# Attention row maxima: from a transpose on TensorE to a round trip through DRAM by DMA

## The chip, the cores and the metric

The kernel runs on one core of a Trainium2 chip. The metric is device time in microseconds of one execution, the median of several. Engines: TensorE (PE in the rows, with its weight loads as PEld), VectorE (DVE), ScalarE (ACT), GpSimd (POOL) and SyncE (SP), which here only issues DMAs.

## The reference

Two sequences of 2048 tokens, width 192, go through a quantised embedding, a layer norm with attention of 12 heads of 64, and a second layer norm with a mixture of small experts. The change is in the attention:

```python
scores = jnp.einsum('bqhe,bkhe->bhqk', q, k) / math.sqrt(D_HEAD)
scores = jnp.where(causal[None, None], scores, -jnp.inf)
pattern = jax.nn.softmax(scores, axis=-1)
z = jnp.einsum('bhqk,bkhe->bqhe', pattern, v)
attn_out = jnp.einsum('bqhe,hed->bqd', z, W_O) + b_O
```

The softmax needs, for each query, the largest score over its keys.

## The kernel before

The attention stage works in 12 units (`UNITS`), one for each pair of heads of each sequence; unit 6 begins the second sequence. Queries are cut into four chunks of 512 (`Q` = 0 to 3), keys into blocks of 128. A unit has two passes. The first pass of unit n projects q, k and v (`project`), and computes scores with queries on the partitions (`score_rows`, items "s1"); VectorE reduces each piece to maxima (`take_maxima`). When a chunk of 512 queries is complete, `maxima` writes the negated maxima, split into a high part and a rest, into columns of the tile `cpad`, one query per partition. `turn_maxima` (item "rows") turns these on TensorE, four 128x128 transposes, and ScalarE copies the 128x512 result into the tile `rows` (it is `zst`), where they lie along the free axis. The second pass (`score_columns`, items "s2") computes the scores again with keys on the partitions; its first matmul of each head multiplies ones with `rows` and so subtracts the maximum of every query. ScalarE takes the exponential (`exponentials`), GpSimd adds the columns up, TensorE multiplies with v (`weigh`).

The first pass of unit n+1 runs as side items inside the second pass of unit n. A unit's second pass has 40 key blocks, taken two at a time in 20 steps (`MACROS`); `sides` says which side items follow the two s2 items of each step. All items of TensorE that fill banks go round a ring of three pairs of PSUM banks (`RING`): item m waits until item m-3 was taken by the engine that reads it. The four "rows" items of a unit are in that ring: three among the s1 items, the fourth (Q = 3) in step 0 of the unit that uses it. The order of every engine is written out by these loops, and all run in order.

SyncE issues the loads in one stream. In its loop, step n loads the weights of unit n+2 and, at n = 5, first `load_x(1)`: the transposed activations of the second sequence into `xt_hi` and `xt_lo`, 1.5 MB in three DMAs. The projections of unit 6 read them; these are the side items of step 1 of unit 5.

Of the kernel before, what the change touches and what calls it, by code (L numbers as in the profile page):

```python
# [60 lines left out]
def tower(nc, x, tok_w, w_q, b_q, w_k, b_k, w_v, b_v, w_o, b_o,  # L61
          f_p, f_c, f_w1, f_b1, f_w2, f_b2, f_g1, f_g1b, f_g2, f_g2b, out, stages=3):
    ctx = ExitStack()
    with ctx:
# [12 lines left out]
        zst = sb("zst", [P, 2, NQ, GTOK], F32R)  # L77
        z_dram = nc.dram_tensor("z_scratch", (2, P, GTOK), F32, kind="Internal").ap()
# [4 lines left out]
        if stages >= 2:  # L83
            stage_attention(nc, w_q, b_q, w_k, b_k, w_v, b_v, w_o, h_all, ident, psum, banks, xT_dram,
                            f_p, f_c, f_w1, f_b1, pm_hi, pm_lo, w1c, zst, z_dram)
# [299 lines left out]
def stage_attention(nc, w_q, b_q, w_k, b_k, w_v, b_v, w_o, h_all, ident, psum, all_banks, xT_dram,  # L385
                    f_p, f_c, f_w1, f_b1, pm_hi, pm_lo, w1c, zst, z_dram):
# [14 lines left out]
    with ExitStack() as own:  # L401
# [21 lines left out]
        cpad = sb("cpad", [P, TQ, P])  # L423
# [13 lines left out]
        raw_c = cpad[:, :, :].rearrange("p t e -> p (t e)")[:, 0:NQ * M].rearrange("p (q m) -> p q m", m=M)  # L437
# [8 lines left out]
        max_taken, c_ready, rows_copied = sem("max_taken"), sem("c_ready"), sem("rows_copied")  # L446
# [16 lines left out]
        TAKEN = {"q": low_taken, "k": low_taken, "v": v_taken, "s1": max_taken, "rows": rows_copied,  # L463
# [12 lines left out]
        def first_pass(n):  # L476

            items = [(kind, n, c) for c in range(2) for kind in "qk"] + [("v", n, c) for c in range(2)]
            for i, c in CHUNKS:
                items.append(("s1", n, i, c))  # L480
                if i % TQ == 0 and i and c == i // TQ:
                    items.append(("rows", n, i // TQ - 1))
            return items

        def sides(it):

            plan = [[] for _ in range(MACROS)]
            plan[0].append(("rows", it, NQC - 1))
# [67 lines left out]
        def _(sp):  # L556
# [34 lines left out]

            load_x(0)
            for n in range(2):
                load_weights(n)
                load_wo(n)
            for n in range(UNITS):
# [13 lines left out]
            sp.wait_ge(filled, place[("rows", LAST, NQC - 1)] + 1)  # L610
# [22 lines left out]
        def _(pool):  # L633
            pool.memset(mask[:, :], 0.0).then_inc(mask_ready, 1)
# [32 lines left out]
        def _(pe):  # L667
# [48 lines left out]
            def turn_maxima(n, Q):  # L716
                banks = slot_free(place[("rows", n, Q)])
                pe.wait_ge(c_ready, n * NQC + Q + 1)
                for t in range(TQ):
                    last = pe.transpose(banks[0][:, t * P:(t + 1) * P], cpad[:, t, :], ident[:, :])  # L720
                last.then_inc(filled, 1)

            def score_columns(it, j):
# [3 lines left out]
                if kt == 0:  # L727
                    pe.wait_ge(rows_copied, it * NQC + Q + 1)
# [67 lines left out]
            def side(item):  # L796
# [6 lines left out]
                elif item[0] == "rows":  # L803
                    turn_maxima(*item[1:])
# [1077 lines left out]
```

## Time and profile before

| | us |
|---|---|
| median of 3 runs | 2665.2 (2664.42 to 2665.51) |
| profiled execution, whole | 2675.88 |
| its span | 2674.1 |
| TensorE busy | 2390.4 |
| VectorE busy | 1856.7 |
| ScalarE busy | 1237.7 |
| GpSimd busy | 1240.0 |
| attention stage | about 236 to 1815 |

A span runs from the first to the last instruction; an engine's busy time is the time in which at least one of its instructions ran. The share of busy time is a mean over three stages; the attention has to be looked at by itself.

### The profile page before, as it was taken

Reading aid. Unit: us, or ns where it says so; the run is one execution under the profiler, and the core shown is the slowest. Engines: PE = TensorE matmul, PEld = TensorE weight load, DVE = VectorE, ACT = ScalarE, POOL = GpSimd, SP = SyncE. Lnnn points to the kernel's source line nnn. Section 1 sums busy time; section 2 is a strip of 40 time slices with the busy share of each in tenths; the row PEclk is TensorE's granted clock in tenths of the full one; section 3 lists DMA queues with packets and bytes.
Section 4 is the critical chain, followed back from the end, with each engine's and each line's share of the span. In section 5 each row is a group of like instructions: output and inputs, shape, how many; then the busy total and the mean of one; then the engine's idle time right before and its main releaser. Section 6 shows DMA issues by size and latency. Waiting matters only on the chain. (4 is left out here: it accounts for less than half of the span.)

```text
span 2674.1 us, 42236 instructions
## 1 busy us (share of the span) xinstructions
PE 2390.4 (89%) x16000; PEld 1225.1 (46%) x16000; DVE 1856.7 (69%) x3768; ACT 1237.7 (46%) x1752; POOL 1240.0 (46%) x858
## 2 busy tenths in 40 slices
PE   2555899999999999999999999996899898998998
PEld 1222465655555555555555556543333333333332
DVE  4782765656565656565555656687888888888987
ACT  3332133333333333333333333355777787777776
POOL 5000166667575757575757666662413413324120
PEclk9877999999999999999999999996999999999999
DMA  1002000000001000000000001131000000000000
GB/s 49 12 13 64 8 8 1 10 1 9 8 2 33 1 10 1 9 1 9 1 9 1 3 1 20 19 52 55 9 19 21 15 19 21 15 19 9 19 7 7
DMA packets 42940, 39.33 MB, mean 15 GB/s; under 512 B 26865, under 2 KB 35186, under 8 KB 41842
## 3 DMA queue, kind: packets, MB, share of 16 engines
q1 hardware_dynamic: 40608, 31.18, 5.2%
q0 software_dynamic: 1536, 3.15, 0.4%
q8 instruction: 127, 2.08, 0.3%
q10 hardware_dynamic: 594, 2.31, 0.2%
q14 instruction: 75, 0.61, 0.1%
HBM read 26.13 MB, written 10.49 MB: 14 GB/s over the span
## 5 line engine op out<-in xcount | busy, mean ns | idle before, releaser
L663 POOL TENSOR_TENSOR acc<-acc,pT 128x1024 f32<-128x1024 f32 (+3 forms) x412 | 836.8, 2031 | 239.9 <-ACT pT L1062 203.5
L1062 ACT ACTIVATE pT<-banks 128x1024 f32<-128x1024 f32 x480 | 407.2, 896 | 811.9 <-PE banks L736 742.2
L1791 DVE TENSOR_TENSOR hw<-hid,banks 128x512 f32<-128x512 f32 x1024 | 663.3, 680 | 93.1 <-PE banks L1475 67.8
L881 DVE TENSOR_REDUCE part<-banks 128x2 f32<-128x1024 f32 (+3 forms) x432 | 438.2, 1044 | 312.0 <-PE banks L712 310.2
L1633 ACT ACTIVATE hid<-banks 128x1024 f32<-128x1024 f32 x512 | 496.8, 1022 | 188.6 <-PE banks L1465 167.3
L752 PE MATMUL banks<-pT,v 128*64 128x512 f32 (+3 forms) x1920 | 405.3, 543 | 1.1 <-POOL pT L647 1.1
L1475 PE MATMUL banks<-wT,select 64*128 64x512 f16 x1024 | 342.3, 395 | 38.2 <-DVE hw L1791 17.2
L1465 PE MATMUL banks<-zst,w1c 50*128 50x512 f32 x1024 | 306.9, 546 | 22.1 <-ACT hid L1633 22.1
L1483 PE MATMUL banks<-hw,w 128*32 128x512 f32 x2048 | 277.9, 615 | 0.8 <-DVE hw L1791 0.8
L1475 PEld LDWEIGHTS banks<-wT,select 64*128 64x128 f16 x1024 | 93.6, 94 | 393.0 <-DVE hw L1791 332.3
L752 PEld LDWEIGHTS banks<-pT,v 128*64 128x64 f32 x1920 | 116.6, 136 | 203.0 <-issue 180.9
L732 PE MATMUL banks<-zst,ones 64*128 64x512 f32 x960 | 199.6, 411 | 2.9 <-DVE h_all L939 2.7
L647 POOL TENSOR_SCALAR_AFFINE_SELECT pT<-pT 128x256 f32<-128x256 f32 x192 | 81.5, 425 | 244.7 <-ACT pT L1062 244.5
L712 PE MATMUL banks<-w1c 64*128 64x512 f32 (+3 forms) x1440 | 177.5, 375 | 10.6 <-DVE part L881 4.8
L736 PE MATMUL banks<-w1c 64*128 64x512 f32 (+3 forms) x1440 | 182.6, 361 | 0.0
L732 PEld LDWEIGHTS banks<-zst,ones 64*128 64x128 f32 x960 | 90.1, 183 | 197.8 <-issue 131.1
L924 DVE RECIPROCAL total<-total 128x256 f32<-128x256 f32 x96 | 167.6, 1746 | 3.1 <-ACT total L1070 2.7
L1375 POOL TENSOR_TENSOR o<-o,h_all 128x768 f32<-128x768 f32 x8 | 14.5, 1818 | 305.7 <-ACT o L1652 305.7
L712 PEld LDWEIGHTS banks<-w1c 64*128 64x128 f32 x1440 | 123.5, 186 | 50.1 <-ACT pT L1062 15.6
L1465 PEld LDWEIGHTS banks<-zst,w1c 50*128 50x128 f32 x1024 | 131.1, 194 | 28.6 <-ACT hid L1633 24.9
L736 PEld LDWEIGHTS banks<-w1c 64*128 64x128 f32 x1440 | 128.5, 185 | 17.9
L885 DVE CUSTOM_DVE_ANT_0 banks<-banks,mask 128x128 f32<-128x128 f32 x384 | 103.5, 312 | 29.3 <-PE banks L712 29.3
(225 smaller groups left out, 3167.3 us busy)
## 6 DMA issues: line engine op xcount, KB each, us to landing
zst<-z_scratch SPq DMA_DIRECT2D x48, 128.0 KB, 4.0
z_scratch<-zp SPq DMA_DIRECT2D x8, 512.0 KB, 2.8
out_h<-o SPq DMA_DIRECT2D x8, 384.0 KB, 2.6
xT_scratch<-xs_hi SPq DMA_DIRECT2D x4, 512.0 KB, 2.7
xt_hi<-xT_scratch SPq DMA_DIRECT2D x2, 1024.0 KB, 5.7
w<-in_L_ffn_W ACTq DMA_DIRECT2D x1, 2048.0 KB, 8.0
xt_hi<-in_L_ffn_W SPq DMA_DIRECT2D x12, 128.0 KB, 4.5
v<-in_L_ffn_W SPq DMA_DIRECT2D x12, 128.0 KB, 4.3
```

The source lines that it names most:

```text
L663: pool.tensor_tensor(acc[:, G % 2, :, off:CH], acc[:, G % 2, :, off:CH], pT[:, slot, :, 0:w], ALU.add).then_inc(summed, 1)
L712: last = pe.matmul(banks[h][:, 0:w], a[u][head(h), i * P:(i + 1) * P], b[u][head(h), c * CH:c * CH + w], start=(k == 0), stop=(k == 2))
L732: pe.matmul(banks[h][:, 0:w], ones[head(h), :], rows[head(h), u, Q, off:CH], start=True, stop=False)
L736: last = pe.matmul(banks[h][:, 0:w], a[u][head(h), kt * P:(kt + 1) * P], b[u][head(h), t0:t0 + w], start=False, stop=(k == 2))
L752: last = pe.matmul(psum[6 + G % 2][head(h), off:CH], v[:, u, kt, head(h)], pT[:, J % PSLOTS, h, 0:CH - off], start=(kt == 0), stop=(j == L ...
L881: last = dve.tensor_reduce(to[:, :, c:c + 1], both[:, :, 0:whole], AX.X, ALU.max)
L1062: act.activation(pT[:, J % PSLOTS, :, 0:CH - off], both[:, :, 0:CH - off], ACT.Exp, scale=E ** -0.5)\
L1465: last = pe.matmul(psum[i], w1[rows, s % NQ, j * P:(j + 1) * P], zst[rows, g % 2, s % NQ, :], start=True, stop=True)
L1475: pe.matmul(bank, select[rows, jr, :], wT[rows, g % 2, s, :], start=True, stop=True).then_inc(spread, 1)
L1483: last = pe.matmul(psum[Y][32 * i:32 * i + 32, :], w2[:, s, j, :], hw[:, n % 2, i, :], start=(n == 0), stop=(n == NSTEP - 1))
L1633: act.activation(hid[:, n % 2, 2 * pair:2 * pair + 2, :], banks[:, pair * 1024:(pair + 1) * 1024].rearrange("p (q n) -> p q n", n=GTOK), A ...
L1791: dve.tensor_tensor(hw[:, n % 2, q, :], hid[:, n % 2, q, :], ring_bank(("w", g, n, q)), ALU.mult).then_inc(mixed, 1)
```

## The change

The "rows" items are gone from TensorE, from ScalarE and from the ring. `maxima` writes its values into a small tile `shift_parts` (two slots, four values for each query of a tile). SyncE stores a slot in DRAM and loads it back in another order, straight into partitions 0, 1, 64 and 65 of `rows`; the other partitions are set to zero once by GpSimd at the beginning. The matmul that uses the rows waits for the load. `raw_c`, which lay in `cpad`, has its own tile, and SyncE no longer waits for the last "rows" item before it loads it.

```diff
+        shift_parts = sb("shift_parts", [P, 2, TQ, 4], F32R)
+        raw_c = sb("raw_c", [P, NQ, M])
...
                 items.append(("s1", n, i, c))
-                if i % TQ == 0 and i and c == i // TQ:
-                    items.append(("rows", n, i // TQ - 1))
...
-            plan[0].append(("rows", it, NQC - 1))
...
+            def turn_maxima(n, Q):
+                G = n * NQC + Q
+                slot, earlier = G % 2, G // 2
+                sp.wait_ge(c_ready, G + 1)
+                sp.dma_start(shift_dram[slot].rearrange("t p k -> p t k"), shift_parts[:, slot, :, :].bitcast(F32))\
+                  .then_inc(parts_stored[slot], 16)
+                sp.wait_ge(parts_stored[slot], 16 * earlier + 16)
+                if n >= 2:
+                    sp.wait_ge(filled, place[("s2", n - 2, NK - 1)] + 1)
+                if earlier:
+                    sp.wait_ge(rows_in[slot], 32 * earlier)
+                else:
+                    sp.wait_ge(rows_cleared, 1)
+                    for h in range(2):
+                        sp.dma_start(rows[h * E:h * E + 2, n % 2, Q, :].bitcast(F32),
+                                     shift_dram[slot, :, :, 2 * h:2 * h + 2].rearrange("t p k -> k (t p)"))\
+                          .then_inc(rows_in[slot], 16)
...
+            for Q in range(NQC):
+                turn_maxima(0, Q)
             for n in range(UNITS):
...
+                if n < LAST:
+                    for Q in range(NQC):
+                        turn_maxima(n + 1, Q)
...
-            sp.wait_ge(filled, place[("rows", LAST, NQC - 1)] + 1)
...
+            pool.memset(rows[:, :, :, :].bitcast(F32), 0.0).then_inc(rows_cleared, 1)
...
                 if kt == 0:
-                    pe.wait_ge(rows_copied, it * NQC + Q + 1)
+                    G = it * NQC + Q
+                    pe.wait_ge(rows_in[G % 2], 32 * (G // 2) + 32)
...
-            pe.wait_ge(consts_ready, 3)
+            pe.wait_ge(consts_ready, 2)
+            pe.wait_ge(rows_cleared, 1)
...
             def maxima(n, Q):
-                if n or Q:
-                    before = ("rows", n, Q - 1) if Q else ("rows", n - 1, NQC - 1)
-                    dve.wait_ge(filled, place[before] + 1)
-                leading, rest = (cpad[:, :, k:k + E + 1:E] for k in range(2))
+                G = n * NQC + Q
+                if G >= 2:
+                    dve.wait_ge(parts_stored[G % 2], 16 * (G // 2))
+                high, rest = (shift_parts[:, G % 2, :, k:k + 3:2] for k in range(2))
...
-            def copy_rows(n, Q):
-                both = item_in(("rows", n, Q))
-                act.activation(rows[:, n % 2, Q, :], both[:, 0, :], ACT.Copy).then_inc(rows_copied, 1)
```

TensorE at the beginning of unit 2, with what each instruction waits for, before the change (L720 is the item "rows", L736 the scores of the second pass, L752 the product with v):

```order
L736 MATMUL banks<-qh,kl 128x384 x2
L720 MATMUL banks<-ident,cpad 128x128 [waits c_ready,max_taken]
L720 MATMUL banks<-ident,cpad 128x128 x3
L752 MATMUL banks<-pT,v 64x256 [waits masked,exp_done]
L752 MATMUL banks<-pT,v 64x256
```

and at the same place in the changed kernel, where L754 stands for L736, L770 for L752 and L750 for L732:

```order
L754 MATMUL banks<-qh,kl 128x384 x2
L770 MATMUL banks<-pT,v 64x256 [waits masked,exp_done]
L770 MATMUL banks<-pT,v 64x256
L770 MATMUL banks<-pT,v 64x128 [waits masked,exp_done]
L770 MATMUL banks<-pT,v 64x128
L784 MATMUL banks<-acc,ones_half 64x512 [waits summed,max_taken]
```

The four transposes and their two waits are gone; nothing stands in their place.

SyncE's stream from the load of the output weights of unit 5 to the second sequence's activations, before:

```order
L579 DMA wo<-in_L_attn_W_O 128x192 [waits ring_filled]
L558 DMA xt_hi<-xT_scratch 128x2048
L560 DMA xt_lo<-xT_scratch 64x1024 x2
L569 DMA w_hi<-in_L_attn_W_Q 128x2x64
L569 DMA w_lo<-in_L_attn_W_Q 64x2x64 x2
```

and in the changed kernel:

```order
L578 DMA wo<-in_L_attn_W_O 128x192 [waits ring_filled]
L596 DMA shift_scratch<-shift_parts 128x4x4 [waits c_ready]
L607 DMA zst<-shift_scratch 2x512x1 [waits rows_in_a,ring_filled,parts_stored_a]
L607 DMA zst<-shift_scratch 2x512x1
L596 DMA shift_scratch<-shift_parts 128x4x4 [waits c_ready]
L607 DMA zst<-shift_scratch 2x512x1 [waits rows_in_b,ring_filled,parts_stored_b]
...
L607 DMA zst<-shift_scratch 2x512x1 [waits rows_in_b,ring_filled,parts_stored_b]
L607 DMA zst<-shift_scratch 2x512x1
L557 DMA xt_hi<-xT_scratch 128x2048 [waits v_taken,low_taken]
L559 DMA xt_lo<-xT_scratch 64x1024 x2
```

The three loads of the activations stand behind the four round trips of unit 5's maxima, and so behind the wait for its last maxima.

## Rows read from the trace of the kernel before

**Rows 1.** Stretch inside the attention (us, then busy us of each engine, granted clock, DMA)
```profile
core 0: us, PE busy (x) PEld busy (x) DVE busy (x) ACT busy (x) POOL busy (x), PEclk, DMA share, GB/s
560.00:680.00 120.00, 117.60 (x830) 69.66 (x830) 72.48 (x131) 39.80 (x50) 77.08 (x54) 1.00 0.03 6
```

**Rows 2.** Groups of instructions by line (busy us, mean ns, idle before, releasers)
```profile
L720 PE MATMUL banks<-ident,cpad 128*128 128x128 f32 x192 | 31.4, 286 | 5.4 <-DVE cpad L900 3.4 <-DVE part L881 2.0
L1053 ACT ACTIVATE zst<-banks 128x512 fp32r<-128x512 f32 x48 | 28.7, 598 | 38.5 <-PE banks L720 38.5
```

**Rows 3.** Timeline of TensorE, steady state (start us, us, what)
```profile
442.91 0.66 PE L720 MATMUL banks<-ident,cpad 128*128 128x128 f32 x4
...
488.40 0.66 PE L720 MATMUL banks<-ident,cpad 128*128 128x128 f32 x4
489.30 0.98 PE L712 MATMUL banks<-w1c 64*128 64x512 f32 x6 [0.25 <-ACT pT L1062]
...
697.01 0.66 PE L720 MATMUL banks<-ident,cpad 128*128 128x128 f32 x4
697.60 0.87 PE L752 MATMUL banks<-pT,v 128*64 128x256 f32 x8
```

**Rows 4.** Waits by engine and line, 440 to 1700 us (total us, times, longest)
```profile
PE banks L712 <- ACT pT L1062: 5.0, 20, 0.3
```

**Rows 5.** Timeline, end of the first pass of unit 0, beginning of its second
```profile
303.94 3.97 DVE L881 TENSOR_REDUCE part<-banks 128x2 f32<-128x1024 f32 x4 [1.23 <-PE banks L712]
...
319.16 0.63 PE L720 MATMUL banks<-ident,cpad 128*128 128x128 f32 x4 [1.90 <-DVE cpad L900]
```

**Rows 6.** Timeline, beginning of unit 5
```profile
950.48 0.18 DVE L900 TENSOR_TENSOR cpad<-negmax,cpad 128x8 fp32r<-128x8 f32 x1
951.00 0.66 PE L720 MATMUL banks<-ident,cpad 128*128 128x128 f32 x4
954.30 1.55 PE L696 MATMUL banks<-xt_hi,w_hi 128*128 128x512 f32 x3
```

**Rows 7.** Timeline of SyncE's queue, the activations of the second sequence
```profile
854.95 0.38 SPq L558 DMA_DIRECT2D xt_hi<-xT_scratch  x1
855.37 1.13 SPq L560 DMA_DIRECT2D xt_lo<-xT_scratch  x2
```

**Rows 8.** DMA issues, 850 to 880 us (KB each, us from issue to landing)
```profile
xt_lo<-xT_scratch SPq DMA_DIRECT2D x2, 256.0 KB, 6.7
wo<-in_L_attn_W_O SPq DMA_DIRECT2D x1, 96.0 KB, 1.8
bk<-in_L_attn_b_K SPq DMA_DIRECT2D x1, 0.5 KB, 2.1
```

**Rows 9.** DMA packets, 481.0 to 481.8 us: only 4-byte ones, of the two bias loads
```profile
DMA packets 208, 0.00 MB, mean 1 GB/s; under 512 B 208, under 2 KB 208, under 8 KB 208
q1 hardware_dynamic: 208, 0.00, 11.9%
```

**Rows 10.** DMA packets, 474.8 to 475.4 us: mostly 256-byte ones, weights
```profile
DMA packets 288, 0.08 MB, mean 127 GB/s; under 512 B 272, under 2 KB 288, under 8 KB 288
q1 hardware_dynamic: 288, 0.08, 53.7%
```

**Rows 11.** TensorE's restart at the beginning of the attention, a stretch as in rows 1
```profile
244.00:254.00 10.00, 6.09 (x9) 2.08 (x10) 0.00 (x0) 0.28 (x1) 0.00 (x0) 0.51 0.31 67
```

**Rows 12.** Timeline of the same beginning, GpSimd and TensorE
```profile
236.28 0.20 POOL L634 MEMSET mask<- 128x128 f32 x1 [188.74 <-POOLq L109]
...
247.91 2.90 PE L696 MATMUL banks<-xt_hi,w_hi 128*128 128x512 f32 x3 [17.73 <-DMA bv_bc<-in_L_attn_b_V]
```

**Rows 13.** Group of instructions: GpSimd's memset of zst in the next stage
```profile
L1302 POOL MEMSET zst<- 32x2048 f32 x2 | 3.6, 1800 | 0.1
```

More of the change, by code:

```diff
@@ L84, in tower @@
             stage_attention(nc, w_q, b_q, w_k, b_k, w_v, b_v, w_o, h_all, ident, psum, banks, xT_dram,
-                            f_p, f_c, f_w1, f_b1, pm_hi, pm_lo, w1c, zst, z_dram)
+                            f_p, f_c, f_w1, f_b1, pm_hi, pm_lo, w1c, zst, z_dram, shift_dram)
         if stages >= 3:
@@ L385, in stage_attention @@
 def stage_attention(nc, w_q, b_q, w_k, b_k, w_v, b_v, w_o, h_all, ident, psum, all_banks, xT_dram,
-                    f_p, f_c, f_w1, f_b1, pm_hi, pm_lo, w1c, zst, z_dram):
+                    f_p, f_c, f_w1, f_b1, pm_hi, pm_lo, w1c, zst, z_dram, shift_dram):
     CH = 512
@@ L445, in stage_attention @@
         hi_done, low_taken, v_taken = sem("hi_done"), sem("low_taken"), sem("v_taken")
-        max_taken, c_ready, rows_copied = sem("max_taken"), sem("c_ready"), sem("rows_copied")
+        max_taken, c_ready, rows_cleared = sem("max_taken"), sem("c_ready"), sem("rows_cleared")
+        parts_stored, rows_in = [sem("parts_stored_a"), sem("parts_stored_b")], [sem("rows_in_a"), sem("rows_in_b")]
         exp_done, masked, summed = sem("exp_done"), sem("masked"), sem("summed")
@@ L462, in stage_attention @@
         CHUNKS = [(i, c) for i in range(KT) for c in range(i // TQ + 1)]
-        TAKEN = {"q": low_taken, "k": low_taken, "v": v_taken, "s1": max_taken, "rows": rows_copied,
+        TAKEN = {"q": low_taken, "k": low_taken, "v": v_taken, "s1": max_taken,
                  "s2": exp_done, "total": total_copied, "out": out_added, "x2": xt_taken, "z": xt_taken}
@@ L590, in load_part @@
                       .then_inc(w1_in[q % 2], 16)
+            def turn_maxima(n, Q):
[11 more added lines that the diff above has]
+                    sp.wait_ge(rows_cleared, 1)
+                with nc.allow_non_contiguous_dma(reason="single values, in the background"):
+                    for h in range(2):
+                        sp.dma_start(rows[h * E:h * E + 2, n % 2, Q, :].bitcast(F32),
+                                     shift_dram[slot, :, :, 2 * h:2 * h + 2].rearrange("t p k -> k (t p)"))\
+                          .then_inc(rows_in[slot], 16)
             load_x(0)
@@ L714, in score_rows @@
                 last.then_inc(filled, 1)
[L716 to L721, printed above, removed]
             def score_columns(it, j):
@@ L802, in side @@
                     make_z()
-                elif item[0] == "rows":
-                    turn_maxima(*item[1:])
                 elif item[0] == "out":
@@ L835, in _ @@
             dve.memset(ones_half[:, :], 1.0).then_inc(consts_ready, 1)
-            dve.memset(cpad[:, :, :], 0.0).then_inc(consts_ready, 1)
             dve.wait_ge(mask_ready, 2)
@@ L892, in maxima @@
             def maxima(n, Q):
-                if n or Q:
-                    before = ("rows", n, Q - 1) if Q else ("rows", n - 1, NQC - 1)
-                    dve.wait_ge(filled, place[before] + 1)
-                leading, rest = (cpad[:, :, k:k + E + 1:E] for k in range(2))
+                G = n * NQC + Q
+                if G >= 2:
+                    dve.wait_ge(parts_stored[G % 2], 16 * (G // 2))
+                high, rest = (shift_parts[:, G % 2, :, k:k + 3:2] for k in range(2))
                 link(dve.tensor_reduce(negmax[:, :], part[:, Q % 2, :, :], AX.X, ALU.max, negate=True))
                 by_tile = negmax[:, :].rearrange("p (t h) -> p t h", h=2)
-                link(dve.tensor_copy(leading.bitcast(F32R), by_tile))
-                dve.tensor_tensor(rest.bitcast(F32R), by_tile, leading, ALU.subtract).then_inc(c_ready, 1)
+                link(dve.tensor_copy(high, by_tile))
+                dve.tensor_tensor(rest, by_tile, high.bitcast(F32), ALU.subtract).then_inc(c_ready, 1)
             def sum_odd(j):
@@ L986, in keep_part @@
                 if q is None:
-                    part, raw = cm[:, :, :], raw_c
+                    part, raw = cm[:, :, :], raw_c[:, :, :]
                 else:
@@ L1091, in side @@
             def side(item):
-                if item[0] == "rows":
-                    copy_rows(*item[1:])
-                elif item[0] == "x2":
+                if item[0] == "x2":
                     take_x2(item[1])
```

5 lines of the change are left out of this document (2 added, 3 removed).

## The prediction

> **What bounds the kernel now.** I read first the stretches of the attention, then the groups of instructions that the change touches, then the timelines around them, and last SyncE's queue and the DMA packets. In a stretch of 120 us in the middle of the attention [rows 1] the reader should see TensorE busy 117.6 us at a granted clock of 1.00, while VectorE has 72.5, ScalarE 39.8 and GpSimd 77.1 us of work. So here the length is TensorE's own list of instructions, and what leaves this list shortens the stage. The unit repeats every (697.01 - 442.91) / 2 = 127.05 us, since these two "rows" items are the same one, two units apart [rows 3].
>
> **What goes.** There are 192 transposes in 48 items, 31.4 us of TensorE, and 48 copies, 28.7 us of ScalarE [rows 2]. The copies lie beside TensorE's work and are worth nothing by themselves. For TensorE not the busy time counts but the place that an item takes: from its start to the next one's start is 697.60 - 697.01 = 0.59 us, call it 0.58 [rows 3]. Three of the 48 items lie in the first pass of unit 0. The other 45 give 45 x 0.58 = 26.1 us. At some of them the next item comes 0.90 us later and not 0.58 (488.40 to 489.30, rows 3), because its bank is still with the exponential; the waits name 20 of these, 5.0 us together, all that this line has between 440 and 1700 us [rows 4]. Without the "rows" item the same bank is asked for one item later, after a longer score item, so I count these 5.0 us as gone too. They could come back before another item; the bound is 0 to 6.
>
> In unit 0 the first pass is held by VectorE, not TensorE. What the item cost there is VectorE's gap of 1.23 us at the third one, and in step 0 of the second pass TensorE's own wait of 1.90 us for `c_ready` [rows 5]. Part of this is taken up by what comes behind; I count 2, bounds 0 to 4. Sum of what goes: 26.1 + 5.0 + 2 = 33 us, bounds 26 and 36.
>
> **What is added and costs nothing.** The GpSimd memset of `zst` holds TensorE by a wait. Two memsets over 2048 columns take 1.80 us each [rows 13], so 4096 columns are 3.6 us from 236.3, done at 240; TensorE begins at 247.91, held by the first loads [rows 12]. It has 8 us of cover. Work of VectorE stays as it was: the two small instructions of `maxima` write another tile. SyncE has room, since a round trip is a store of 512 packets and two loads of 1024. A rows load is due early: those of chunks 0 to 2 are asked for in the next unit, those of chunk 3 in step 12 of 20, some 75 us behind `c_ready`. The load of the experts' weights moves behind the last round trip, from unit 10 to the beginning of unit 11, and is wanted in its steps 8 and 9, about 50 us later, so it is covered too unless the round trips are several times longer than below.
>
> **What is added and lies on the path.** SyncE's stream is in order, and `load_x(1)` now stands behind the round trip of unit 5's last maxima. Before, it was issued at 854.95 [rows 7], 99 us ahead of the projections that read it. Now it can't be issued before the maxima are ready at 950.66, and the projection of unit 6 is asked for at 954.30 - 0.58 = 953.7 [rows 6]. TensorE is in order, so everything stands behind it: unit 5's scores, and with them ScalarE and GpSimd. Step by step:
> - The store: a load of 128 small packets lands in 2.1 us [rows 8]; 384 more packets at 0.6 us / 288 = 2.1 ns [rows 10] are 0.8 us. It lands at 953.6.
> - The two loads of single values: no DMA of before is like this one (2 partitions, 1024 packets of 4 bytes each). The nearest row is the 4-byte packets of the bias loads, 208 in 0.8 us, or 3.85 ns each over all engines [rows 9]: 2048 of them are 7.9 us. From below: their busy share is 11.9%, that is 0.119 x 16 x 800 / 208 = 7.3 ns of an engine per packet, so that 16 engines could do 2048 in 0.9 us. From above: one engine saw such a packet every 16 x 800 / 208 = 61.5 ns, and if few engines carry them they take up to 63 us (below). I take 7.9, the row of the same size of packet.
> - The activations, issued at about 954.8: before, the second `xt_lo` was issued at 855.9 and landed 6.7 us later [rows 7, 8], 7.7 us behind the first issue. By themselves they land at 962.5; behind the packets, in the same queue, at 970.4. I take the second.
> - So TensorE stands 970.4 - 953.7 = 16.7 us, bounds 8.8 and 50 and more.
> - The clock: at the beginning of the attention, after a wait of 17.73 us, TensorE worked from 247.91 to about 254 at the lower level, 1.2 GHz (clock 0.51 in that stretch), before it was back at 2.4 [rows 11, 12]. Six microseconds at half are 3 lost; I count 3, bounds 0 and 5.
>
> **The sum.** -33 + 16.7 + 3 = -13.3 us. Against the profiled execution, 2675.9, that is 2662.6; that execution was 10.7 us above the median of the runs, 2665.2, and against this I forecast **2652 us**. Its own range: 2638 (36 gone, 8.8 of stall, no clock) to 2660.
>
> **How many engines carry the single values.** The loads' destination has two partitions, and the before kernel has none like it: its smallest has 16. The Trainium skill (DMA: Bandwidth & Descriptors, "Why a DMA increments its semaphore by 16 and not by 1") says that a DMA is spread over the largest number up to 16 that divides the slowest dimension of both patterns: here 2. No run here shows it yet. By that rule each round trip gives two engines 1024 packets each; at the 7.3 ns of busy time [rows 9] this is 7.5 us, as in my sum, and at the pace an engine showed with 16 in use it is the rival below.
>
> **The rivals.**
> - *A longer stall, gain given back.* The packets of single values take T instead of 7.9 us, for want of engines or for HBM reads that wait for each other; the stall is 8.8 + T. From T = 21 us (8.8 + 21 + 3 = 33), or 20 ns a packet on two engines, the kernel isn't faster any more. At T = 30 it is 2665.2 - 33 + 38.8 + 3 = 2674 us. For it: 256-byte packets come every 16 x 600 / 288 = 33 ns on an engine at the densest [rows 10]. Against: they were busy 17.9 ns of it, 4-byte ones only 7.3.
> - *The round trips become the bound (slower).* Place: SyncE's queue in every unit. It decides from the point at which four round trips take more than a unit of 127 us, T = 31.8 us, or 31 ns a packet on two engines. At 33 ns, T = 34.1 and a unit takes 136.5, 9.5 more for some 11.5 units: 2775 us. At 61.5 ns, T = 63, 252 us a unit, +1440: 4100 us. For it: the pace of rows 9, and the rule above. Against: the bias loads were only 8 packets per engine, so the pace holds their start and end.
> - *The activations aren't held up by the packets.* The stall is 8.8, and the time 2665.2 - 33 + 8.8 + 3 = 2644 us. For it: engines that the single values don't use are free; against: the load is done only when its last share is.
> - *TensorE's freed time is not used.* Another engine or a bank wait takes the place; then only the stall remains, 2665.2 + 20 = 2685 us. Against it speak 77 of 120 us as the highest load of another engine [rows 1].
>
> **How the numbers follow.** My forecast 0.42, the short stall 0.10, the long stall 0.25, the round trips as the bound 0.17, the unused time 0.06. A difference under 0.2% (5.3 us, so 2660 to 2670.5) can't be told from none. Faster: 0.40 of the forecast, all of the short stall, 0.01 of the long: 0.51. Same: the rest of the forecast and 0.13 of the long stall: 0.16. Slower: 0.33. The range reaches from 2638 to 2680, which leaves out the round trips as the bound and the end of the unused time.
>
> **What would show it.** Right: no transposes of maxima on TensorE, units of 127.05 - 2.9 = 124.1 us; one idle time of TensorE of about 17 us before L720 (the projection) near 930 us, ended by the DMA of `xt_hi` or `xt_lo`; behind it some microseconds at the lower clock; the loads of `zst` from the scratch landing 8 to 12 us after their issue; no wait of the scores (L750) for them. Wrong: waits of L750 in every unit (the second rival), a single stall of 30 us or more (the first), units that stay at 127 us (the last).

## The result and the profile after

The changed kernel takes 2670.7 us (median of 20 runs, 2666.1 to 2674.3), the kernel before 2665.2 (20 runs beside them): a ratio of 1.0017, 95% interval 1.001 to 1.0024. It is a little slower, by about as much as a measurement can tell. The forecast was 2652.

The page of the kernel after, its head and busy times:

```profile
span 2670.0 us, 41959 instructions
PE 2375.1 (89%) x15808; PEld 1215.9 (46%) x15808; DVE 1867.8 (70%) x3767; ACT 1212.7 (45%) x1704; POOL 1245.2 (47%) x859
```

TensorE's busy time fell by 15 us and ScalarE's by 25, and the span by 4. (The spans flatter the change: in the execution profiled before the first projection began at 247.91 us [rows 12], after at 237.2, and the embedding stage ahead of it is the same in both.) Since TensorE works in order, I cut its timeline at the first projection of each unit, the same instruction every time:

```profile
430.52 1.12 PE L720 MATMUL banks<-xt_hi,w_hi 128*128 128x512 f32 x2
557.06 1.12 PE L720 MATMUL banks<-xt_hi,w_hi 128*128 128x512 f32 x2
682.12 1.13 PE L720 MATMUL banks<-xt_hi,w_hi 128*128 128x512 f32 x2
808.77 1.13 PE L720 MATMUL banks<-xt_hi,w_hi 128*128 128x512 f32 x2
```

The reader should see units of 126.5, 125.1 and 126.7 us where before had 127.0 [rows 3] and the forecast 124.1. One unit is far longer, 144.6 us (808.77 to 953.40), the one with the load of the second sequence. There TensorE's timeline, SyncE's queue and the landings (KB each, us from issue to landing) read:

```profile
935.29 0.28 PE L754 MATMUL banks<-qh,kl 64*128 64x128 f32 x2
953.40 3.42 PE L720 MATMUL banks<-xt_hi,w_hi 128*128 128x512 f32 x4 [17.84 <-issue]
```
```profile
932.44 0.36 SPq L596 DMA_DIRECT2D shift_scratch<-shift_parts  x1
935.41 4.01 SPq L607 DMA_DIRECT2D zst<-shift_scratch  x2
939.53 4.13 SPq L557 DMA_DIRECT2D xt_hi<-xT_scratch  x1
943.70 1.16 SPq L559 DMA_DIRECT2D xt_lo<-xT_scratch  x2
```
```profile
xt_hi<-xT_scratch SPq DMA_DIRECT2D x1, 1024.0 KB, 9.8
xt_lo<-xT_scratch SPq DMA_DIRECT2D x2, 256.0 KB, 7.9
```

That is the stall of the forecast, 17.8 us for 16.7. Its inside differs: the two loads of single values hold the queue for 4.0 us while they are issued, and the issue behind them, of the activations, is held another 4.1 us, where the same one took 0.38 before [rows 7]. (In the diff ahead the two loads look as if they stood in the `else` branch. They are issued for every chunk, four times a unit.)

The waits of TensorE in the attention, 300 to 1750 us (total us, times, longest):

```profile
PE banks L795 <- DVE part L897: 23.6, 11, 2.2
PE banks L720 <- issue: 17.8, 1, 17.8
PE banks L736 <- DVE part L897: 7.8, 11, 0.7
PE banks L795 <- DVE oT L947: 1.8, 1, 1.8
```

No wait of L750 for the rows: the round trips are hidden, as forecast. The waits for ScalarE of [rows 4] are gone too. But there is one wait a unit of 2.1 us at the output (L795), and one of 0.7 at a score item (L736). The kernel before waited at the same output, 15.8 us in 11 units, at most 1.5 us. My text ahead had not looked at that line. This is one of these waits, first after, then before:

```profile
488.31 1.84 PE L736 MATMUL banks<-w1c 64*128 64x512 f32 x18
492.28 2.93 PE L795 MATMUL banks<-wo,oT 128*128 128x192 f32 x8 [2.13 <-DVE part L897]
```
```profile
504.92 1.84 PE L712 MATMUL banks<-w1c 64*128 64x512 f32 x18
508.21 1.57 PE L777 MATMUL banks<-wo,oT 128*128 128x192 f32 x8 [1.45 <-DVE part L881]
```

The same eight matmuls take 2.93 us for 1.57. Stretches of the kernel after around this place (columns as in [rows 1]) show why:

```profile
488.30:491.70 3.40, 1.84 (x20) 1.35 (x16) 3.30 (x6) 1.24 (x2) 2.87 (x2) 1.00 0.08 2
491.70:495.10 3.40, 2.82 (x8) 2.42 (x8) 2.16 (x6) 0.00 (x0) 1.85 (x1) 0.56 0.11 1
```

The granted clock is near the lower of the two levels, 1.2 GHz, in the second stretch. Such a drop of 3.4 us, each worth some 1.6 us, stands in nine of the ten units between 305 and 1588 us; before had none there. In steady state a unit with a drop takes 126.5 to 126.7 us, the one without 125.1.

What VectorE did before that output, with GpSimd beside it:

```profile
486.61 0.20 DVE L913 TENSOR_REDUCE negmax<-part 128x8 f32<-128x40 f32 x1
486.84 1.48 DVE L915 CAST shift_parts<-negmax 128x8 fp32r<-128x8 f32 x1
488.36 0.17 DVE L916 TENSOR_TENSOR shift_parts<-negmax,shift_parts 128x8 fp32r<-128x8 f32 x1
488.44 1.75 DVE L940 RECIPROCAL total<-total 128x256 f32<-128x256 f32 x1
490.22 0.69 DVE L947 TENSOR_TENSOR oT<-banks,total 128x512 f32<-128x512 f32 x1
491.00 2.36 DVE L897 TENSOR_REDUCE part<-banks 128x2 f32<-128x1024 f32 x2
```
```profile
483.38 4.91 POOL L687 TENSOR_TENSOR acc<-acc,pT 128x1024 f32<-128x1024 f32 x2 [0.91 <-ACT pT L1074]
```

Read it backwards. The output is item m of the ring and needs the banks of item m-3, a score item that VectorE frees with the first L897 reduction, at about 492.2. Ahead of it in VectorE's order stand the multiply, the reciprocal and the three small operations on the maxima. The CAST of 128x8 values takes 1.48 us and ends at 488.32, just as the second of GpSimd's two additions in that row does (483.38 + 4.91 = 488.29). At the same place before, the same CAST took 0.60 us:

```profile
503.65 0.60 DVE L899 CAST cpad<-negmax 128x8 fp32r<-128x8 f32 x1
```

Why did it collide now and not before? `sides` spreads the items of the next unit's first pass evenly over 16 steps, by their number. The change took three "rows" items out of that list, so 40 items are cut instead of 43, and score items that had nothing to do with the change moved by a step. Step 8 had (6,1), (7,0), (7,1) and has (7,0), (7,1); step 7 got (6,1). Item (7,1) completes chunk 1, and the maxima of chunk 1 are turned right behind it. They come sooner against GpSimd's addition, and the CAST is held by more of it.

### The profile page after: what moved, and what is told of

It reads as the page before. It is cut to its first block and busy times, and to the rows that moved or that the text cites. A ratio compares the mean times of both kernels' runs of the same rounds, so it can differ in the third digit from the quotient of the medians.

```text
span 2670.0 us, 41959 instructions
## 1 busy us (share of the span) xinstructions
PE 2375.1 (89%) x15808; PEld 1215.9 (46%) x15808; DVE 1867.8 (70%) x3767; ACT 1212.7 (45%) x1704; POOL 1245.2 (47%) x859
## 5 line engine op out<-in xcount | busy, mean ns | idle before, releaser
L897 DVE TENSOR_REDUCE part<-banks 128x2 f32<-128x1024 f32 (+3 forms) x432 | 437.2, 1044 | 295.5 <-PE banks L736 293.2
L770 PE MATMUL banks<-pT,v 128*64 128x512 f32 (+3 forms) x1920 | 410.6, 549 | 1.1 <-POOL pT L671 1.1
L770 PEld LDWEIGHTS banks<-pT,v 128*64 128x64 f32 x1920 | 118.1, 138 | 205.1 <-issue 170.8
L750 PE MATMUL banks<-zst,ones 64*128 64x512 f32 x960 | 200.0, 412 | 3.2 <-DVE h_all L955 2.7
L736 PE MATMUL banks<-w1c 64*128 64x512 f32 (+3 forms) x1440 | 177.2, 377 | 13.2 <-DVE part L897 9.0
L754 PE MATMUL banks<-w1c 64*128 64x512 f32 (+3 forms) x1440 | 182.9, 362 | 0.0
L750 PEld LDWEIGHTS banks<-zst,ones 64*128 64x128 f32 x960 | 90.1, 184 | 199.0 <-issue 129.3
L736 PEld LDWEIGHTS banks<-w1c 64*128 64x128 f32 x1440 | 124.4, 188 | 52.9 <-DVE part L897 18.7
L754 PEld LDWEIGHTS banks<-w1c 64*128 64x128 f32 x1440 | 128.3, 185 | 18.4
L720 PE MATMUL banks<-xt_hi,w_hi 128*128 128x512 f32 x192 | 98.5, 637 | 35.7 <-issue 17.8
```

What stands on the lines that cost most here:

```text
L736: last = pe.matmul(banks[h][:, 0:w], a[u][head(h), i * P:(i + 1) * P], b[u][head(h), c * CH:c * CH + w], start=(k == 0), stop=(k == 2))
L750: pe.matmul(banks[h][:, 0:w], ones[head(h), :], rows[head(h), u, Q, off:CH], start=True, stop=False)
L754: last = pe.matmul(banks[h][:, 0:w], a[u][head(h), kt * P:(kt + 1) * P], b[u][head(h), t0:t0 + w], start=False, stop=(k == 2))
L770: last = pe.matmul(psum[6 + G % 2][head(h), off:CH], v[:, u, kt, head(h)], pT[:, J % PSLOTS, h, 0:CH - off], start=(kt == 0), stop=(j == L ...
L897: last = dve.tensor_reduce(to[:, :, c:c + 1], both[:, :, 0:whole], AX.X, ALU.max)
```

## The experiments

All are compared with the kernel before on the same chip. In the names, x is the second sequence's activations, and the cut is the way in which the list of side items is divided over the steps; the numbered parts below explain each. Units are steady ones (a unit with a drop, where most have one), read as above. The drops are counted in the ten units from the first projection of unit 1 to that of unit 11; two that begin with the start of the first of these (in kept ahead and in before, new cut) are left out. The twelve kernels ahead of the last two ran where before took 2665 to 2666 us. For the last two before took 2676.4, and their own traces begin the attention at 248.7 and 250.2 us where the others have 236 to 239, so about 11 us more lie ahead of the attention, as in the execution profiled before. There the ratio counts.

| kernel | us | ratio, 95% interval | unit, us | drops in ten units |
|---|---|---|---|---|
| the changed kernel | 2670.7 | 1.0017 [1.001, 1.0024] | 126.6 | 9 |
| x ahead | 2652.8 | 0.9954 [0.994, 0.9967] | 126.6 | 8 |
| x between | 2657.5 | 0.9968 [0.9956, 0.998] | 126.6 | 6 |
| loads doubled | 2678.2 | 1.0048 [1.0034, 1.0061] | 126.6 | 6 |
| items kept | 2666.0 | 1.0002 [0.9993, 1.0011] | 127.0 | 0 |
| kept ahead | 2634.1 | 0.9882 [0.9867, 0.9897] | 124.1 | 0 |
| kept behind | 2661.6 | 0.9984 [0.9975, 0.9993] | 126.6 (128.2 with a drop) | 2 |
| old cut, x ahead | 2630.7 | 0.9869 [0.9854, 0.9884] | 124.2 | 0 |
| outputs later | 2627.4 | 0.9859 [0.9844, 0.9874] | 123.9 | 0 |
| no cast | 2652.4 | 0.9955 [0.9941, 0.9968] | 126.7 | 8 |
| old cut alone | 2650.3 | 0.995 [0.9936, 0.9964] | 124.2 | 0 |
| before, new cut | 2696.8 | 1.0117 [1.0102, 1.0133] | 129.7 | 9 |
| before, outputs later | 2642.6 | 0.9924 [0.991, 0.9938] | 125.05 | 0 |
| maxima behind | 2619.6 | 0.9784 [0.977, 0.9797] | 122.3 | 0 |
| outputs later, old cut | 2621.1 | 0.9787 [0.9774, 0.9801] | 122.4 | 0 |

**1. The stall: x ahead, x between, loads doubled.** The load of the second sequence moves ahead of unit 5's round trips; or between the last `c_ready` and its store; or stays, and each load of single values runs twice, the second time into an unused tile.

```diff
-                    if n == NP - 1:
-                        load_x(1)
...
+                if n == NP - 2:
+                    sp.wait_ge(low_taken, 4 * n + 8)
+                    sp.wait_ge(v_taken, 2 * n + 4)
+                    load_x(1)
                 if n < LAST:
                     for Q in range(NQC):
```

> The changed kernel with one move in SyncE's stream: the three loads of the second sequence's activations stand ahead of the four round trips of unit 5, behind the load of the output weights, as early as before. Theory (the stall of 17.8 us and the 1.5 us of slower matmuls behind it come from that place alone): both go, 2670.6 - 19.3 = 2651 us, up to 2653 if unit 5 gets the short clock drop that its neighbours have. Rival (the gain is lost to the DMA traffic or spread over the units): 2662 or more.

> The changed kernel, with the activations loaded behind the wait for unit 5's last maxima, but ahead of their round trip. This parts the stall in two. Theory (the wait for the maxima costs the rest, the packets of the round trip and SyncE's blocked issue the most): TensorE stands 5 to 6 us and not 17.8, the time is 2670.6 - 12 = 2658 us. Rival (the order against the packets does not matter, only the late issue): the stall stays above 12 us, 2666 us or more.

> The changed kernel with every load of single values done twice, the second time into an unused tile. Theory (the activations queue behind the packets, some 8 us per round trip; in all other units the round trips are hidden): the one stall grows from 17.8 to about 26 us, the units stay as they are, 2678 us. Rival 1 (packets of other loads do not hold the activations): 2671. Rival 2 (the packets cost the other units something): units longer than 126.7 us, 2690 or more.

All three came out as expected: 2652.8, 2657.5 and 2678.2. With x ahead TensorE's long wait is gone and no other wait changes by more than 0.5 us. Between, it is shorter; doubled, longer:

```profile
939.27 3.75 PE L722 MATMUL banks<-xt_hi,w_hi 128*128 128x512 f32 x4 [4.97 <-issue]
```
```profile
959.56 3.75 PE L728 MATMUL banks<-xt_hi,w_hi 128*128 128x512 f32 x4 [25.26 <-issue]
```

So two loads of 1024 single values cost 25.26 - 17.84 = 7.4 us, where the forecast took 7.9 for them. Doubled, they delay no other unit: four round trips don't come near a unit's length. The stall is worth 2670.65 - 2652.84 = 17.8 us. With x ahead the kernel should then have been at about 2632, had the forecast's other terms held; 20 us were still missing.

**2. Is it the items? Items kept, kept ahead, kept behind.** x ahead in all three, and at the places of the old items TensorE does four transposes of `ident` into the item's bank and ScalarE copies them to an unused tile. Kept are all four of a unit; those of chunks 3 and 0; those of chunks 1 and 2.

```diff
+                if i % TQ == 0 and i and c == i // TQ and i // TQ - 1 in KEPT:
+                    items.append(("rows", n, i // TQ - 1))
...
+            if NQC - 1 in KEPT:
+                plan[0].append(("rows", it, NQC - 1))
```

> The kernel of e1 with the items put back on TensorE and ScalarE: four transposes of the identity and a copy into an unused tile at the old places, waiting for the maxima as before, while the rows come by DMA. Theory (the DMA path is free in itself; the short clock drops belong to the new order of TensorE): units of 127.0 us as before, no drops in the attention, 2665 us. Rival (the DMA traffic brings the clock drops or slows TensorE): drops in the units, 2675 us or more.

> The kernel with the activations loaded first and the rows by DMA, with the unused transposes and copies kept at two of the four places of a unit only: chunks 3 and 0, the two that lie ahead of step 9, where TensorE waits for VectorE before the output item. Theory (freed time ahead of step 9 makes that wait longer, 2.13 against 1.45 us, and the short clock drop follows a wait of that length): the wait is 1.5 us again, no drops, units of about 125.8 us, 2652 us. Rival (the drops come from fewer instructions on TensorE as such, or at other places): drops in most units, 127 us a unit, 2662 or more.

> The same with the unused transposes and copies kept at the other two places, chunks 1 and 2, which lie behind step 9. Theory: the wait of step 9 stays 2.1 us and the drops stay, units of about 127.8 us, 2665 us. Rival: no drops, units of about 126, 2652 us.

With all four kept the time and the unit are those of before, and no clock drops: with x ahead the DMA path itself costs TensorE nothing. But kept ahead gave 2634.1, 19 us faster than none kept, where 2652 was expected and 2662 or more by the rival. An item that costs 0.58 us can't save 1.7 us a unit. What the edit also does is to change the number of items in the list, 41 here. That cut puts (7,1) into step 9, the step of the output itself, three items ahead of it. So the output needs the banks of (7,1), which VectorE frees before it turns the maxima, and the wait falls from 2.1 us to this:

```profile
616.04 1.57 PE L811 MATMUL banks<-wo,oT 128*128 128x192 f32 x8 [0.16 <-DVE part L919]
```

Kept behind missed too. Its list has 42 items, and (7,1) stays in step 8, but (8,0) joins it there. The wait of 2.1 us was expected to stay, with the drops, and 2665 us. Instead there are two shorter waits close together in each unit, 0.71 and 1.23 us, and the time is 2661.6. Two of the ten units have the drop even so. This is one of them; in the others the same eight matmuls take 1.54 us:

```profile
618.35 0.50 PE L745 MATMUL banks<-kh,qh 64*128 64x512 f32 x2 [0.71 <-DVE part L915]
620.83 2.49 PE L811 MATMUL banks<-wo,oT 128*128 128x192 f32 x8 [1.23 <-DVE oT L965]
```

**3. The cut by itself.** The items stay gone; placeholders stand in the list where they were, and are dropped after cutting. With x ahead, and as the only edit of the changed kernel. And the reverse in the kernel before: its score items cut as the change cuts them, the "rows" items behind the same score items as ever.

```diff
                 items = first_pass(it + 1)
+                for Q in range(NQC - 1):
+                    items.insert(items.index(("s1", it + 1, TQ * (Q + 1), Q + 1)) + 1, None)
...
-                    plan[t] += rest[a:z]
+                    plan[t] += [item for item in rest[a:z] if item]
```

> The kernel with the activations first, and with the score items of the first pass at exactly the steps where they stood before the change (the list is cut as if the three removed items were still in it). Theory (the place of the score items plays no part, VectorE's lateness in step 9 does): wait of step 9, drops and time as with the activations first, 2653 us. Rival (the new cut is what brings the drops): no drops, units of 125.0 us, 2639 us.

> The changed kernel with one edit: the score items of the next unit are issued at the steps where they stood before the change (x stays behind the round trips, as changed). Theory (the two losses are separate and add): the cut is worth 2652.84 - 2630.69 = 22.2 us with x ahead, of which the ten or so drops of the clock; the long stall of unit 5 stays at 17.8 us, so 2670.7 - 22 = 2648.5, faster than before by 0.6%. Rival (the gain of the old cut is bound to x being ahead): 2665 to 2671.

> The kernel before with one edit, the other way round: its 40 score items are cut into the 16 steps without counting the three items that turn the maxima, as the change cuts them; these stand behind the same score items as ever. Nothing is removed. Theory (the new cut alone makes VectorE late at step 9, since its cast meets the beginning of GpSimd's addition): the wait of 1.45 us becomes 2.1 and the clock drops behind it in most units, 11 times 0.7 plus about 10 times 1.6, so 2665.5 + 22 = 2687. Rival (the items that turn the maxima give VectorE the slack there, and the new cut hurts only without them): 2665.

With x ahead it is the rival that was right, and by more than it asked for: 2630.7, 22.2 us under x ahead. As the only edit it gives 2650.3, 20.3 us under the changed kernel and 0.5% under before. In the kernel before the new cut costs 31.7 us, more than the 22 expected, and brings the drops with it. There the wait of 2.1 us, and the drop behind it, stand at the "rows" item just ahead of the output; the expectation had left out the second wait, 0.7 us a unit. The three agree in sign: the cut of the score items costs 20 to 32 us, with or without the change that brought it. The waits of the kernel with the old cut and x ahead:

```profile
PE banks L799 <- DVE part L901: 15.7, 11, 1.4
PE banks L799 <- DVE oT L951: 10.4, 12, 1.8
```

At the same output VectorE's cast is 0.61 us long, and the stretches around it keep the higher clock, although TensorE still waits 1.4 us there:

```profile
484.34 0.61 DVE L919 CAST shift_parts<-negmax 128x8 fp32r<-128x8 f32 x1
```
```profile
485.60:489.00 3.40, 1.96 (x21) 1.45 (x17) 3.33 (x5) 1.26 (x2) 2.86 (x2) 1.00 0.08 2
489.00:492.40 3.40, 3.40 (x18) 1.80 (x20) 2.45 (x6) 0.00 (x0) 1.87 (x1) 1.00 0.21 6
```

**4. The chain on VectorE: no cast, maxima behind.** x ahead and the new cut in both. One writes the high part with a maximum of the row with itself instead of a copy; the other turns the maxima of chunks 0 to 2 one score item later.

```diff
-                link(dve.tensor_copy(high, by_tile))
+                link(dve.tensor_tensor(high, by_tile, by_tile, ALU.max))
```
```diff
-                if diagonal and t == TQ - 1:
+                if c == 0 and t == 0 and Q or (i, c) == (KT - 1, NQC - 1):
                     dve.wait_ge(max_taken, nth[("s1", n, i, c)] + 1)
-                    maxima(n, Q)
+                    maxima(n, (i - 1) // TQ)
```

> x ahead of the round trips and the new cut, with one edit: VectorE writes the high part of the negated maxima with a maximum of the row with itself (a TENSOR_TENSOR, as the one that follows it, 0.17 us) instead of a copy (CAST). In the kernel with x ahead and the copy, the CAST of chunk 1 took 1.48 us and ended with GpSimd's addition, and TensorE waited 2.1 us for a pair of banks behind it, after which the clock dropped for 3.4 us. Theory (the cast holds VectorE until GpSimd's addition is over, that makes the wait long, and the long wait brings the drop): the wait falls to some 0.8 us, 1.3 us a unit less over 11 units (14), and the drops go, 9 to 11 times 1.6 us (14 to 18): 2652.8 - 28 to 32, thus 2621 to 2625. Rival (the new cut is late by its own load, and the kind of the instruction doesn't matter): 2653.

> x ahead of the round trips and the new cut, with one edit: VectorE turns the maxima of chunks 0 to 2 into their two parts one score item later, behind the first score item of the next chunk instead of ahead of the reciprocal and the multiply on which the output rests. Theory (the three operations, 0.20 + 1.48 + 0.17 us with their gaps 1.9 us, stand on VectorE ahead of all that the output's banks wait for; the copy is held until GpSimd's addition ends; the wait of 2.1 us that this makes brings the drop of the clock): the wait at the output falls by up to 1.9 us a unit and the drops go, so the unit of 126.65 comes down to 123.2 to 124 and the time to 2620 to 2628. Rival (the drops come from something else in that step, such as its load or GpSimd's addition beside it): the wait goes but the drops stay, 2652.5 - 4 to 21, thus 2632 to 2648.

The first changed nothing (2652.4): my theory that the copy is the kind that is held fell. The operation in its place is held just as long, until GpSimd's addition is over (484.12 + 4.91 = 489.03):

```profile
487.55 1.50 DVE L917 TENSOR_TENSOR shift_parts<-negmax 128x8 fp32r<-128x8 f32 x1
489.09 0.17 DVE L918 TENSOR_TENSOR shift_parts<-negmax,shift_parts 128x8 fp32r<-128x8 f32 x1
489.17 1.75 DVE L942 RECIPROCAL total<-total 128x256 f32<-128x256 f32 x1
```
```profile
484.12 4.91 POOL L689 TENSOR_TENSOR acc<-acc,pT 128x1024 f32<-128x1024 f32 x2 [0.92 <-ACT pT L1076]
```

The second, with the same operations, the same cut and the same number of instructions, took the unit from 126.6 (125.0 without a drop) to 122.3 us, the ratio from 0.9954 to 0.9784. The wait at the output is 0.4 us and no clock drops any more:

```profile
PE banks L797 <- DVE part L899: 4.5, 11, 0.4
PE banks L752 <- DVE h_all L957: 2.7, 2, 2.1
PE banks L797 <- DVE oT L949: 1.8, 1, 1.8
```

That is 45 us of the 2665, more than the 25 to 33 expected; again the expectation had left out the 0.7 us wait at a score item, which went too (7 us), and what lies behind the ten units gained as well (from the first projection of unit 11 to the end it is 1079.5 us for 1086.3). The list of operations is as it was; only what stands ahead of the freeing reduction moved, and both the wait and the drop went with it. One thing did change beside the order: at their new places the CASTs are held for less, 10.3 us in all for 39.0 with x ahead, so this run alone doesn't part the wait from the load. The next one does.

**5. The outputs later.** x ahead, and the output items of chunks 0 to 2 one step later, at the head of the step; the same in the kernel before; and with the old cut on top.

```diff
-        OUT_BEHIND = [4] * LAST + [6]
+        OUT_BEHIND = [5] * LAST + [6]
...
-                    plan[t].append(("out", it, Q))
+                    plan[t].insert(len(plan[t]) if it == LAST else 0, ("out", it, Q))
```

> The kernel with the activations first, and the output items of chunks 0 to 2 one step later and at the head of their step, where their bank was taken long before. Theory (the wait before the output item is lost time of TensorE and brings the drop): both go, 125.0 - 2.1 = 122.9 us a unit, 11 units: 2653 - 11 x 3.2 = 2618 us. Rival (VectorE is late for the score items too, so the wait moves to the next item): units above 124.5, 2640 or more.

> The kernel before with the output items of chunks 0 to 2 one step later and at the head of the step, in all units but the last, as was done to the changed kernel with x ahead (which this took from 2652.8 to 2627.4). Control: how much of that gain is there without the change. In the trace of before the outputs wait 15.8 + 3.4 + 1.8 = 21 us for banks, no clock drops stand in the attention, so at most 20 us can go: 2645 to 2650. Theory (the change is worth its 1.6 to 2 us a unit once nothing waits at the outputs): it ends some 18 to 22 us above 2627.4, at 2647. Rival (the gain of the kernel with outputs later came from the outputs alone and the change adds nothing): 2627.

> The best of what was found put together: x ahead of the round trips, the outputs one step later, and the score items at their steps of before. The kernel with the outputs later has waits of 0.70 and 0.28 us a unit left, both for VectorE's reductions, and the one with the old cut has neither. Theory (both go): 2627.4 - 11 x 0.98 = 2616.6. Rival (TensorE is at its own pace once no wait is over 1 us, or others take their place): 2625 to 2628.

With x ahead it took the time to 2627.4, between theory and rival: the output's waits and the drops are gone, two waits of 0.7 and 0.3 us a unit for VectorE's reductions are left. VectorE is as busy as with x ahead here (1867.2 us for 1867.9) and its CASTs are held as long (38.8 us for 39.0, 1.49 at this place). So the drops go with TensorE's wait, not with the load of that step. The kernel before gains too, 22.5 us (2642.6), where at most 20 were expected: 19 of the 21 us that its outputs had waited are gone, and 2.7 us of waits for ScalarE. With the old cut nothing waits in the middle of a unit, and the ratio is 0.9787. By the ratios that is 19 us under outputs later, for the 11 expected; the units are 1.5 us shorter for waits of 1.0, and where the other half comes from is open. Its longest line of waits for VectorE's reductions is this:

```profile
PE banks L740 <- DVE part L901: 2.2, 5, 1.0
```

This kernel and maxima behind are the fastest of the study, 2.1% under before; between them the measurement sees no difference.

The kernel before with the outputs later, and the changed one with the outputs later and the old cut, are also the cleanest measure of the change itself. They have the same cut, the same place of the outputs, and no waits of note; a steady unit of each, before first:

```profile
558.69 1.13 PE L696 MATMUL banks<-xt_hi,w_hi 128*128 128x512 f32 x2
683.84 1.13 PE L696 MATMUL banks<-xt_hi,w_hi 128*128 128x512 f32 x2
```
```profile
561.80 1.12 PE L724 MATMUL banks<-xt_hi,w_hi 128*128 128x512 f32 x2
684.20 1.12 PE L724 MATMUL banks<-xt_hi,w_hi 128*128 128x512 f32 x2
```

125.15 against 122.40. Over nine steady units the means are 125.05 and 122.40: 2.65 us a unit, for the 2.9 of the forecast.

## Why the prediction was wrong

Its sum had the terms -33 (what goes), +16.7 (the stall) and +3 (its clock). Each has a measured partner:

- *What goes, -33:* from all items kept to items gone with the old cut, x ahead in both, 2666.0 - 2630.7 = 35.3 us. Right in size. The stretch of unit 0 gave 4.6 us (72.9 to 68.3), of which 0.6 is its fourth item, so 4.0 where the forecast had 2. The 5.0 us of bank waits did go, as counted. What the parts leave out is that the outputs now wait for `oT`, 10.4 us for 1.8, so their agreement is in part luck.
- *The stall with its clock, +19.7:* with the old cut, x late against x ahead, 2650.3 - 2630.7 = 19.6 us; with the new cut 17.8. Right in size. Of its parts, the clock's share varies: in the changed kernel the first four matmuls behind the stall took 3.42 us for 1.98, 1.5 us lost and not 3; with the old cut the unit behind the stall is 2.6 us longer than its neighbours (126.8 for 124.2). The loads of single values cost 7.4 us for 7.9, but how they take it is not as in the forecast. In a dense stretch, 937 to 940 us, the profile of the changed kernel counts

```profile
DMA packets 1002, 0.00 MB, mean 1 GB/s; under 512 B 1002, under 2 KB 1002, under 8 KB 1002
q1 hardware_dynamic: 1002, 0.00, 18.8%
```

so one packet every 3.0 ns over all engines, each busy 0.188 x 16 x 3000 / 1002 = 9.0 ns and not 7.3, with 3.0 of them under way at a time. The Trainium skill's rule from the prediction (DMA: Bandwidth & Descriptors, "Why a DMA increments its semaphore by 16 and not by 1") gives two engines for each load. Two engines that take one packet after the other at 9 ns would need 9.2 us for 2048 packets; here either the packets overlap in an engine or the two loads of a pair are on different engines, and the trace doesn't say which. That 7.5 us came near is luck. The pace of 61.5 ns, on which the slow rival stood, was only that of a short load's start and end. What I had not seen is where the time is spent: SyncE's queue itself stands, in the issue of these loads and of the next one.
- *Missing, +20.3:* the new cut (2670.65 - 2650.34). This is the step that failed, a term that the sum has at nothing without giving a reason. The sum counted an item's place on TensorE and took it that "what leaves this list shortens the stage"; it held the other items to be where they were. The text ahead says of the side items only that `sides` places them. The comparison of the two instruction streams would have shown the score items moving by a step, and the waits of the kernel before that its outputs already stood 1.5 us behind VectorE in every unit. Either was to be had without a run.

The sum with it is -35.3 + 19.6 + 20.3 = +4.6, for +5.4 measured. The three differences form one chain of kernels, from items kept to the changed one, so they must add up to the distance between these two; what the sum tests is only that items kept is where before is. And the changed kernel with the old cut, the one that the forecast really described, took 2650.3 us for a forecast of 2652.

The chances have a slip: by their parts Same is 0.02 + 0.13 = 0.15 and Slower 0.34, not 0.16 and 0.33.

The rivals: the long stall, the round trips as the bound and the short stall are refuted by the stall of 17.8 us and by the doubled loads. The one on freed time that isn't used, with a chance of 0.06, named a bank wait as what could take the place, and a bank wait is what came. But it held the freed time to be lost, and that was not so: the items' 35 us came off, and the new cut took 20 back. I argued against it with VectorE's and GpSimd's busy shares, 72 and 77 of 120 us. These say nothing of a chain of 6 us in which one waits for the other in each unit, and they hardly grew: in the stretch of [rows 1] GpSimd has 77.5 us after for 77.1, VectorE 76.6 for 72.5. The price named there, 2685, stood for no gain at all; in truth 2.4 us a unit were taken back: against the kernel with the old cut (124.2 us) a unit has 2.1 + 0.7 us of waits for 1.4 + 0.8, and the drop's 1.6, which is 2.2 of the 2.4.

What each of these is worth alone is not separated fully. That the drops follow the waits, and not the load of the step, is shown by outputs later, where the load stays and both go, and by before, new cut, where the long wait stands at another item and the drop comes behind it. Which waits bring one is not settled. One of 2.1 us does in most units but not in all: in the changed kernel's unit from 557 to 682 us the wait is 2.15 us and the clock stays at 1.00, and x between and loads doubled have the same waits and 6 drops in ten units. One of 1.4 us did in none, and the pair of 0.71 and 1.23 us of kept behind did in two of ten. Why is open.

## What to carry to other kernels

When a change takes items out of a list that a rule spreads over steps, the other items move: compare the instruction streams of every engine before adding up prices, and look at who waits next to the moved ones, however short the wait. On an in-order engine what a consumer waits for may be a small operation ahead of the one that frees its buffer; move that one behind, and the wait goes without any work being saved (here 45 us by moving three operations one item on). When a DMA with many tiny pieces goes into a shared queue, put the large transfers ahead of it.

## What the runs showed of the hardware

- *A small VectorE operation is held until GpSimd's running addition ends.* The CAST of 128x8 values takes 0.17 us alone and up to 1.58 beside GpSimd's TENSOR_TENSOR of 128x1024 (2.4 us each). In the seven traces looked at (before, the changed kernel, x ahead, old cut with x ahead, no cast, kept behind, maxima behind) every one that began while such an addition ran ended 0.02 to 0.04 us behind its end. A TENSOR_TENSOR with two SBUF inputs in its place was held as long (1.50); the one behind it, in GpSimd's gap between two additions, was not (0.17). The reduction, the reciprocal (SBUF) and the multiply that reads PSUM, beside the same additions, kept their 0.20, 1.75 and 0.69 us. The Trainium skill (GPSIMD Engine Reference, Specifications) says that GpSimd's SBUF interfaces are shared with VectorE and contend with VectorE instructions that have two SBUF inputs or run in a two-port mode, and (SBUF — State Buffer, Terms) that the port pair is held for a whole instruction while the loser blocks. The trace agrees, with up to 1.4 us for 8 values per partition.
- *The issue of a DMA was held behind loads of many tiny pieces.* A pair of loads, each of 1024 four-byte pieces into two partitions, took SyncE's queue 4.0 us to issue, and the issue behind them 4.1 us for 0.38 before; doubled, the second pair took 9.2 us:

```profile
933.79 4.48 SPq L610 DMA_DIRECT2D zst<-shift_scratch  x2
938.32 9.20 SPq L614 DMA_DIRECT2D unused<-shift_scratch  x2
947.63 4.20 SPq L559 DMA_DIRECT2D xt_hi<-xT_scratch  x1
```

- *TensorE's clock can fall to its lower level behind a single wait of 2 us in the middle of dense work.* In the changed kernel TensorE is busy 117.0 of the 120 us from 560 to 680; behind its waits of 2.1 us the granted clock was 0.56 in a stretch of 3.4 us, about 1.6 us lost, in nine of ten units. Behind waits of 1.4 us in the same place there was none in ten units (old cut, x ahead), behind 0.71 and 1.23 us close together there were two (kept behind).
